# Loading V's weights on ScalarE's DMA queue instead of SyncE's, with four more idle products before the first transposes

## The chip, the cores and the metric

One core of a Trainium2 chip runs the whole program in one launch. The metric is the device time of that core in microseconds (us). The kernel before takes 897.44 us, the median of three runs that lie between 897.3 and 897.68 us.

## The reference: what is computed

The input x has 4 sequences of 512 tokens with 512 features. All arithmetic is float32.

```
xn = layernorm(x)                                # over the 512 features, no weights
q, k, v = xn @ wq.T, xn @ wk.T, xn @ wv.T        # 16 heads of q, 4 of k and v, 128 each; rope on q and k
per head, over chunks of tokens (linear attention with decay exp(-lam * distance)):
    o  = (q k^T * decay) v + (q * q_decay) kv
    kv = blk * kv + (k * k_decay)^T v
s = o @ wo.T
g = silu(mlp(xn))    # mlp: silu(xn @ gate * gs) * (xn @ up * us), then @ down * ds; weights rounded to fp8
out = x + s * g
```

## The kernel before, in words

Every matrix product is made from two or three passes over split operands: each float32 operand is split into a high part (a rounding cast by ScalarE) and a low part (the rest, by VectorE or GpSimd). The program has five instruction streams written out by hand, one for each engine, in a fixed order, and they meet at semaphores. No scheduler reorders them.

The stretch that the change touches is the first 30 us. The first sequence comes in four tiles of 128 tokens (`load_x`, into `stage`). For each tile VectorE takes statistics (`tile_stats`, L841), makes mean and variance (`mean_var`, L847 and L849), and after a power by GpSimd (`power`, L1285) the reciprocal deviation (`inv_std`, L857 to L863), and normalizes (`norm`, L876). The two tiles 0 and 1 form the first group, but VectorE's stream has `tile_stats(2)` between `mean_var(0)` and `inv_std(0)`. TensorE then turns each tile with four products against the identity `ident` (`ln_transpose`, L1428); ScalarE casts the turned tile (`norm_hi`, L576), VectorE makes its low part (`norm_lo`, L883). V's weights arrive in four pieces of 128 x 512 in `wv_raw`, which lies in the tile `f_all`. ScalarE casts them (`wv_split_hi`, L638), one piece ahead of `norm_hi(0)` and three behind it, and VectorE makes the low parts (`wv_split_lo`, L950). TensorE multiplies: `v_first_high` (L1392) for tiles 0 and 1 needs the casts of all four weight pieces and of the tile; `v_first_low` and `v_first_rest` (L1372) follow.

Ahead of the first transposes TensorE does `WARM` idle products on a zeroed tile, and `WARM_MORE` = 4 behind the second one; their results are never used. They are issued by this code (L1408):

```
pe.wait_ge(warm_d, 1)
warm_up(WARM)
pe.wait_ge(ident_sem, 16)
ln_transpose(0)
ln_transpose(1)
warm_up(WARM_MORE)
v_first_high(0)
v_first_high(1)
```

All loads and stores are issued by SyncE in one queue, in the order in which its stream is written: x tiles 0 to 3, `ident`, V's weights (L396), x tiles 4 to 7, the first pieces of the MLP's weights. Tiles 6 and 7 wait there until the `stage` slots of tiles 0 and 1 have been turned.

Of the kernel before, what the change touches and what calls it, by code (L numbers as in the profile page):

```python
# [17 lines left out]
KT = D // P  # L18
# [63 lines left out]
    for half in range(2):  # L82
        VD_AT[2 + (t + half) // MT, (t + half) % MT] = (x, half)
AW_FROM = 6
WARM = 14
WARM_MORE = 4


# [6 lines left out]
def attention_mlp_kernel(nc, x_nat, x_t, attn_w, wv_tab, out_w, mlp_w, scales, rope_tab, decay_tab, q_decay_tab,  # L95
                         k_decay_tab, ident_in, out):
    ctx = ExitStack()
    with ctx:
# [59 lines left out]
        wv_raw = f_all[:, MT - KT:MT, :]  # L158
# [95 lines left out]
        wv_in = [sem(f"wv_in{k}") for k in range(KT)]; wv_hi = sem("wv_hi"); wv_lo = sem("wv_lo")  # L254
# [49 lines left out]
        def _(sp):  # L304
# [87 lines left out]
            for i in range(TT):  # L392
                load_x(i)
            sp.dma_start(ident[:], ident_in).then_inc(ident_sem, 16)
            for k in range(KT):
                sp.dma_start(wv_raw[:, k, :], wv_tab[:, k, :]).then_inc(wv_in[k], 16)  # L396
            for i in range(TT, 2 * TT):
                load_x(i)
            load_piece(0)
# [172 lines left out]
        def _(act):  # L572
# [63 lines left out]
            def wv_split_hi(k):  # L636
                act.wait_ge(wv_in[k], 16)
                act.copy(wv[:, 0, k, :], wv_raw[:, k, :]).then_inc(wv_hi, 1)  # L638
# [15 lines left out]
            def vd_round(x, half):  # L654
                for g in (2 * half, 2 * half + 1):
# [3 lines left out]
                        act.wait_ge(vd_out[y % 2], 16 * (y // 2))  # L659
                    act.copy(vd_split[:, y % 2, 0, :], vd_sb[:, y % 2, :]).then_inc(vd_hi, 1)  # L660

            act.preload_act_table(ACT.Silu)
            wv_split_hi(0)
            norm_hi(0)
# [703 lines left out]
        def _(pe):  # L1368
# [36 lines left out]
            def warm_up(count):  # L1405

                for _ in range(count):
                    pe.matmul(bank[7][:], acc[:, 0, 0, 0:P // 2].bitcast(BF16), acc[:, 0, 0, 0:S // 2].bitcast(BF16),  # L1408
                              start=True, stop=True)
# [68 lines left out]
# [3 lines that stand above are left out]
# [272 lines left out]
```

## Time and profile before

| | |
|---|---|
| median of three runs | 897.44 us |
| the profiled execution's own time | 898.68 us |
| its span, first to last instruction | 896.9 us |
| TensorE busy in the span | 889.6 us (99%) |
| VectorE, ScalarE, GpSimd busy | 656.1, 409.5, 370.4 us |
| mean granted TensorE clock | 0.998 |

The profiled execution took 1.24 us longer than the median, and 1.8 us of it lie outside the span. A busy share near 99% says that TensorE nearly always had an instruction in flight; what it lacks are a few us, so the places to look at are those in which it is idle or runs at a lower clock.

### The profile page before, as it was taken

How to read it: one execution, taken by the hardware profiler on the slowest of the kernel's cores; microseconds unless marked ns; L12 is line 12 of the kernel's file. 1: busy time of each engine (PE TensorE's matmuls, PEld its weight loads, DVE VectorE, ACT ScalarE, POOL GpSimd, SP SyncE). 2: the span in 40 equal slices, each digit the busy share in tenths (PEclk: the TensorE clock that was granted, in tenths of full speed). 3: DMA queues.
4: the chain of work that ended last, by engine and by line, in shares of the span. 5: the costliest groups of instructions: out<-in, count | busy, mean ns of one | idle time of the engine just before them, and what ended most of it. 6: DMA issues, size and time to landing. Idle time of an engine off the chain costs nothing.

```text
span 896.9 us, 12455 instructions
## 1 busy us (share of the span) xinstructions
PE 889.6 (99%) x4060; PEld 735.0 (82%) x4060; DVE 656.1 (73%) x941; ACT 409.5 (46%) x683; POOL 370.4 (41%) x273
## 2 busy tenths in 40 slices
PE   8999999999999999999999999999999999999998
PEld 5888888888888888888888888888888888888887
DVE  6988896787643257766777867677767678788798
ACT  2544343443533455445355454463554544634442
POOL 1012112122122475536545456365454563553546
PEclk9999999999999999999999999999999999999999
DMA  6694414389650534522544614345335064273854
GB/s 215 187 390 167 171 48 164 141 307 328 244 211 1 212 125 147 186 80 108 187 126 156 220 39 175 102 175 194 101 144 181 18 221 160 99 259 103 295 135 169
DMA packets 86922, 150.08 MB, mean 167 GB/s; under 512 B 38480, under 2 KB 59616, under 8 KB 81504
## 3 DMA queue, kind: packets, MB, share of 16 engines
q1 hardware_dynamic: 86880, 149.55, 48.7%
q8 instruction: 23, 0.38, 0.2%
q14 instruction: 19, 0.16, 0.1%
HBM read 103.38 MB, written 46.15 MB: 167 GB/s over the span
## 4 chain that ended last, share of the span: by engine, by line
PE 91%; issue 3%; DVE 3%; POOL 2%; DMA 0%; ACT 0%; SPq 0%; DVEq 0%; POOLq 0%; ACTq 0%
PE bank L1372 90%; POOL d_r L1308 1%; POOL rot L1317 1%; DMA stage<-in_x_nat 0%; PE bank L1392 0%; DVE d_sb L1164 0%; DVE tail_sb L1217 0%; DVE d_sb L1116 0%; DVE tail_sb L1215 0%; DVE d_r L1191 0%; PE bank L1428 0%; DVE acc L1211 0%; PE bank L1408 0%; DVE o_r L1170 0%; DVE tail_sb L1201 0%
## 5 line engine op out<-in xcount | busy, mean ns | idle before, releaser
L1372 PE MATMUL bank<-xn,aw 128*128 128x512 f32 x960 | 229.1, 390 | 0.0
L1317 POOL TENSOR_TENSOR rot<-rot 128x512 f32<-128x512 f32 x80 | 126.7, 1583 | 233.4 <-DVE rot L1103 233.4
L1372 PEld LDWEIGHTS bank<-xn,aw 128*128 128x128 f32 x960 | 179.0, 188 | 37.4 <-issue 0.7
L1372 PE MATMUL bank<-o_r,ow 128*128 128x512 f32 (+1 forms) x792 | 184.5, 383 | 0.2 <-DVE o_r L1170 0.2
L1308 POOL TENSOR_TENSOR d_r<-d_sb,d_r 128x512 fp32r<-128x512 f32 x126 | 165.5, 1336 | 37.0 <-ACT d_r L762 36.9
L1372 PE MATMUL bank<-xn,gu_w 128*128 128x512 f32 x768 | 179.6, 389 | 0.0
L1372 PEld LDWEIGHTS bank<-o_r,ow 128*128 128x128 f32 x792 | 145.5, 188 | 29.8 <-issue 0.6
L1372 PEld LDWEIGHTS bank<-xn,gu_w 128*128 128x128 f32 x768 | 144.2, 188 | 29.9
L1102 DVE TENSOR_TENSOR rot<-bank,rope 128x512 f32<-128x512 f32 x80 | 55.2, 690 | 100.2 <-ACT rot L747 100.1
L746 ACT COPY rot<-bank 64x512 f32<-64x512 f32 x80 | 46.8, 584 | 156.9 <-PE bank L1372 156.6
L762 ACT CAST d_r<-d_sb 128x512 fp32r<-128x512 f32 x128 | 78.9, 621 | 83.2 <-DVE d_sb L1164 60.7
L1291 POOL TENSOR_TENSOR fsplit<-f_all,fsplit 128x512 fp32r<-128x512 f32 x36 | 49.0, 1366 | 129.1 <-ACT fsplit L620 129.1
L1372 PE MATMUL bank<-fsplit,dn_w 128*128 128x512 f32 x384 | 93.8, 390 | 0.0
L1372 PEld LDWEIGHTS bank<-fsplit,dn_w 128*128 128x128 f32 x384 | 71.8, 188 | 15.5 <-issue 0.3
L1116 DVE TENSOR_TENSOR d_sb<-rot,q_decay 128x256 f32<-128x256 f32 x64 | 83.6, 1324 | 1.2 <-POOL rot L1317 1.2
L1164 DVE TENSOR_TENSOR d_sb<-bank,decay 128x512 f32<-128x512 f32 x96 | 64.0, 684 | 22.5 <-PE bank L1372 21.5
L1372 PE MATMUL bank<-q_r,k_r 128*128 128x512 f32 x288 | 78.5, 391 | 0.0
L1372 PE MATMUL bank<-d_r,v_r 128*128 128x512 f32 (+1 forms) x336 | 76.8, 361 | 0.1
L1372 PEld LDWEIGHTS bank<-d_r,v_r 128*128 128x128 f32 x336 | 57.7, 188 | 13.1 <-POOL d_r L1308 2.3
L1372 PEld LDWEIGHTS bank<-q_r,k_r 128*128 128x128 f32 x288 | 52.9, 188 | 10.7 <-DVE q_r L1109 0.6
L735 ACT CAST q_r<-rot 128x512 fp32r<-128x512 f32 x64 | 39.8, 622 | 40.1 <-POOL rot L1317 39.0
L945 DVE SCALAR_TENSOR_TENSOR f_all<-bank,scale_sb,f_all 128x512 f32<-128x512 f32 x36 | 26.9, 748 | 41.5 <-PE bank L1372 36.0
(91 smaller groups left out, 948.9 us busy)
## 6 DMA issues: line engine op xcount, KB each, us to landing
xn<-xn_split SPq DMA_DIRECT2D x15, 2048.0 KB, 7.8
v_decayed<-vd_split SPq DMA_DIRECT2D x32, 512.0 KB, 3.2
vd_r<-v_decayed SPq DMA_DIRECT2D x16, 1024.0 KB, 7.0
v_r<-v_split SPq DMA_DIRECT2D x16, 512.0 KB, 3.5
wst<-in_mlp_w SPq DMA_DIRECT2D x10, 768.0 KB, 6.6
xn_split<-xn SPq DMA_DIRECT2D x3, 2048.0 KB, 13.3
stage<-in_x_t SPq DMA_DIRECT2D x20, 256.0 KB, 5.0
stage<-in_attn_w SPq DMA_DIRECT2D x4, 1280.0 KB, 5.5
```

The costliest lines, as they stand in the source:

```text
L735: act.copy(dst, rot1[:, r % RRING, :]).then_inc(qk_hi, 1)
L746: act.copy(rot2[0:ROT, r % RRING, :], ps[ROT:, :])
L762: act.copy(d_r[:, slot(e), 0, :], d_sb[:, slot(e), :]).then_inc(d_hi, 1)
L945: dve.scalar_tensor_tensor(out=f, in0=gu_ps[(2 * u + 1) % 3][:], scalar=scale_sb[:, MT + m:MT + m + 1], in1=f, op0=ALU.mult, op1=ALU.mult) ...
L1102: dve.tensor_tensor(rot1[:, r % RRING, :], proj_bank(n, r)[:], rope[:, 0, :], ALU.mult)
L1116: dve.tensor_tensor(d_sb[:, slot(e), bass.ts(h % 2, HALF)], rot1[:, (h + 1) % RRING, HALF:S], q_decay[:, h, :], ALU.mult).then_inc(q_decay ...
L1164: dve.tensor_tensor(by_head(d_sb[:, slot(e), :]), by_head(sc_ps[t % TRING][:]), decay[:, h0:h0 + nh, i0 - j:i0 - j + ni, :], ALU.mult).the ...
L1291: pool.tensor_tensor(fsplit[:, e % FRING, 1, :], src, fsplit[:, e % FRING, 0, :].bitcast(F32), ALU.subtract).then_inc(f_lo, 1)
L1308: pool.tensor_tensor(d_r[:, slot(e), 1, :], d_sb[:, slot(e), :], d_r[:, slot(e), 0, :].bitcast(F32), ALU.subtract).then_inc(d_lo, 1)
L1317: pool.tensor_tensor(rot1[:, r % RRING, :], rot1[:, r % RRING, :], rot2[:, r % RRING, :], ALU.add).then_inc(qk_sum, 1)
L1372: last = pe.matmul(dst, a, b, start=start and x == 0, stop=stop and x == len(pairs) - 1)
```

## The change

`WARM` goes from 14 to 18. SyncE's stream no longer issues the four loads of V's weights; ScalarE's stream issues them as its first instructions, ahead of its table load. No wait is added or removed.

```
-WARM = 14
+WARM = 18
             for i in range(TT):
                 load_x(i)
             sp.dma_start(ident[:], ident_in).then_inc(ident_sem, 16)
-            for k in range(KT):
-                sp.dma_start(wv_raw[:, k, :], wv_tab[:, k, :]).then_inc(wv_in[k], 16)
             for i in range(TT, 2 * TT):
                 load_x(i)
             load_piece(0)
...
+            for k in range(KT):
+                act.dma_start(wv_raw[:, k, :], wv_tab[:, k, :]).then_inc(wv_in[k], 16)
             act.preload_act_table(ACT.Silu)
             wv_split_hi(0)
             norm_hi(0)
```

SyncE's stream from its start, before and now (`f_all` is where V's weights land, `stage` takes the x tiles), as the difference:

```order
 L310 DMA stage<-in_x_nat 128x512 x4
 L394 DMA ident<-in_ident 128x128
-L396 DMA f_all<-in_wv_tab 128x512 x4
 L310 DMA stage<-in_x_nat 128x512 x4
 L338 DMA wst<-in_mlp_w 128x512 x2
```

The four weight loads are gone, and x tiles 4 and 5 stand right behind the identity. ScalarE's stream from its start, before (its table load, then the weight casts around the first cast of x):

```order
0 L571 UNCONDITIONAL_BRANCH
1 L662 ACT_TABLE_LOAD
2 L638 CAST wv<-f_all 128x512
3 L576 CAST xn<-bank 128x4x128
4 L638 CAST wv<-f_all 128x512 x3
5 L576 CAST xn<-bank 128x4x128 x3
```

And now, the same stretch of ScalarE:

```order
0 L569 UNCONDITIONAL_BRANCH
1 L661 DMA f_all<-in_wv_tab 128x512 x4
2 L662 ACT_TABLE_LOAD
3 L636 CAST wv<-f_all 128x512
4 L574 CAST xn<-bank 128x4x128
5 L636 CAST wv<-f_all 128x512 x3
6 L574 CAST xn<-bank 128x4x128 x3
```

The four issues come first; the casts keep their order, with three weight casts still behind the first cast of x. On TensorE only the count of the first group of idle products differs.

## Rows read from the trace of the kernel before

**Rows 1.** The page: busy time of the span, and the chain by line.

```profile
PE 889.6 (99%) x4060; PEld 735.0 (82%) x4060; DVE 656.1 (73%) x941; ACT 409.5 (46%) x683; POOL 370.4 (41%) x273
...
PE 91%; issue 3%; DVE 3%; POOL 2%; DMA 0%; ACT 0%; SPq 0%; DVEq 0%; POOLq 0%; ACTq 0%
```

**Rows 2.** Waits of TensorE from 26.2 us to the end: total, times, longest.

```profile
PE bank L1372 <- DVE o_r L1170: 0.2, 1, 0.2
```

**Rows 3.** Stretches: length, busy of each engine, PEclk, DMA share, GB/s.

```profile
0.00:9.20 9.20, 5.76 (x18) 2.29 (x19) 4.47 (x13) 1.90 (x2) 1.05 (x7) 1.00 0.72 234
9.20:9.30 0.10, 0.10 (x3) 0.10 (x2) 0.10 (x1) 0.00 (x0) 0.00 (x0) 0.89 0.96 369
9.30:12.60 3.30, 3.30 (x12) 2.17 (x10) 2.90 (x11) 2.62 (x5) 0.70 (x1) 0.50 0.81 253
12.60:12.70 0.10, 0.10 (x2) 0.06 (x1) 0.10 (x1) 0.00 (x0) 0.00 (x0) 0.54 0.52 164
```

**Rows 4.** Timeline of TensorE's start: start, length, instruction, count, idle before.

```profile
1.47 5.35 PE L1408 MATMUL bank<-acc 128*128 128x512 bf16 x14 [1.47 <-DVE acc L989]
8.79 1.49 PE L1428 MATMUL bank<-ident,stage 128*128 128x128 f32 x8 [1.97 <-DVE stage L876]
10.07 1.91 PE L1408 MATMUL bank<-acc 128*128 128x512 bf16 x4
11.43 2.79 PE L1392 MATMUL bank<-wv,xn 128*128 128x512 f32 x8
14.05 1.03 PE L1428 MATMUL bank<-ident,stage 128*128 128x128 f32 x8
```

**Rows 5.** Timeline of TensorE's weight loads for the first idle products.

```profile
5.29 0.15 PEld L1408 LDWEIGHTS bank<-acc 128*128 128x128 bf16 x1 [0.28 <-issue]
5.71 0.61 PEld L1408 LDWEIGHTS bank<-acc 128*128 128x128 bf16 x3 [0.28 <-issue]
```

**Rows 6.** Timeline of VectorE, 5.2 to 8.9 us.

```profile
5.43 0.69 DVE L841 BATCH_NORM_STATS2 stats<-stage 128x6 f32<-128x512 f32 x1 [0.82 <-DMA stage<-in_x_nat]
...
6.52 0.69 DVE L841 BATCH_NORM_STATS2 stats<-stage 128x6 f32<-128x512 f32 x1
7.51 0.16 DVE L857 TENSOR_TENSOR rs<-rs 128x2 f32<-128x2 f32 x1 [0.31 <-POOL rs L1285]
...
8.10 1.00 DVE L876 TENSOR_SCALAR stage<-stage,mv,rstd 128x512 f32<-128x512 f32 x2
```

**Rows 7.** Timeline of ScalarE, 8 to 13 us.

```profile
8.44 0.62 ACT L638 CAST wv<-f_all 128x512 fp32r<-128x512 f32 x1 [6.41 <-DMA f_all<-in_wv_tab]
9.46 0.59 ACT L576 CAST xn<-bank 128x512 fp32r<-128x512 f32 x1 [0.41 <-PE bank L1428]
9.95 1.66 ACT L638 CAST wv<-f_all 128x512 fp32r<-128x512 f32 x3
11.51 0.58 ACT L576 CAST xn<-bank 128x512 fp32r<-128x512 f32 x1
```

**Rows 8.** Timeline of SyncE's issues from the start.

```profile
0.75 1.82 SPq L310 DMA_DIRECT2D stage<-in_x_nat  x4
2.61 0.43 SPq L394 DMA_DIRECT2D ident<-in_ident  x1
3.09 1.92 SPq L396 DMA_DIRECT2D f_all<-in_wv_tab  x4
```

**Rows 9.** DMA issues one by one, in order of issue: size, us to landing.

```profile
stage<-in_x_nat SPq DMA_DIRECT2D x1, 256.0 KB, 3.1
...
stage<-in_x_nat SPq DMA_DIRECT2D x1, 256.0 KB, 4.2
...
stage<-in_x_nat SPq DMA_DIRECT2D x1, 256.0 KB, 4.4
...
stage<-in_x_nat SPq DMA_DIRECT2D x1, 256.0 KB, 5.4
...
ident<-in_ident SPq DMA_DIRECT2D x1, 64.0 KB, 5.2
...
f_all<-in_wv_tab SPq DMA_DIRECT2D x1, 256.0 KB, 5.5
...
f_all<-in_wv_tab SPq DMA_DIRECT2D x1, 256.0 KB, 5.8
```

**Rows 10.** Stretches, for the DMA engines: columns as in Rows 3.

```profile
2.00:7.00 5.00, 4.82 (x14) 1.59 (x12) 2.19 (x6) 0.03 (x1) 0.24 (x1) 1.00 0.85 254
7.00:10.00 3.00, 1.21 (x8) 1.24 (x9) 2.54 (x9) 1.16 (x3) 0.48 (x1) 0.88 1.03 388
```

More of the change, by code:

```diff
@@ L84 @@
 AW_FROM = 6
-WARM = 14
+WARM = 18
 WARM_MORE = 4
@@ L394, in _ @@
             sp.dma_start(ident[:], ident_in).then_inc(ident_sem, 16)
-            for k in range(KT):
-                sp.dma_start(wv_raw[:, k, :], wv_tab[:, k, :]).then_inc(wv_in[k], 16)
             for i in range(TT, 2 * TT):
@@ L660, in vd_round @@
                     act.copy(vd_split[:, y % 2, 0, :], vd_sb[:, y % 2, :]).then_inc(vd_hi, 1)
+            for k in range(KT):
+                act.dma_start(wv_raw[:, k, :], wv_tab[:, k, :]).then_inc(wv_in[k], 16)
             act.preload_act_table(ACT.Silu)
```

## The prediction

> **What bounds the kernel now.** I read the page first. TensorE is busy for 889.6 of 896.9 us and carries 91% of the chain that ended last; DMA and ScalarE have 0% of it [rows 1]. So only what moves TensorE's stream can move the end. Then I asked for TensorE's waits behind the stretch that the change touches: from 26.2 us on there is one, of 0.2 us [rows 2]. From there TensorE is the bound without a gap, and whatever is won or lost before 26.2 us is carried to the end one to one. I look for no second effect there.
>
> Before it, TensorE's timeline has two losses [rows 4]. The 14 idle products run from 1.47 to 6.82 us, then the engine stands for 1.97 us until VectorE has normalized tile 0, and the first transposes start at 8.79 us. The granted clock then falls from 1.00 (2.4 GHz) to 0.50 (1.2 GHz) near 9.3 us and stays there until just short of 12.7 us [rows 3]. Four idle products take 1.91 us in that stretch [rows 4]. At the very start the clock column says 1.00, but the loads of the idle products come 0.42 us apart (5.29 to 5.71) and only the last three stand within 0.61 us [rows 5]. So they too ran at the lower level until about 5.8 us, and an idle product costs about 0.43 us before and 0.21 us behind that point.
>
> What does the first transpose wait for? Going back: normalizing starts at 8.10, the last steps of the deviation at 7.51, and between them and the statistics of tile 1 (5.43, which waited for its tile) stand the statistics of tile 2 at 6.52 [rows 6]. So the chain is x tile 1, then x tile 2, then VectorE. Landing times are issue [rows 8] plus time to landing [rows 9]; the issues are some 0.47 us apart. X tiles 0 to 3 land at 3.9, 5.4, 6.1 and 7.6 us, the identity at 7.8, V's weight pieces at 8.4 (the start of the cast that waited for it, [rows 7]), 9.1, 9.7 and 10.3.
>
> **The change part by part.** *The weight loads come sooner.* ScalarE waited 6.41 us for the first piece, the largest wait at the start, and it looks like the prize. It is not on the path. That cast ends at 9.06, and ScalarE then waits another 0.41 us for TensorE's transposes before it casts x tile 0 at 9.46 [rows 7]. The other three weight casts stand behind that cast in ScalarE's stream, at 9.95 and after, back to back for 1.66 us. Pieces 2 to 4 had landed at 9.1, 9.7 and 10.3, each before its cast. Earlier weights are worth 0.0 us.
>
> *The four issues on ScalarE* should take what they take on SyncE, 1.92 us [rows 8], from about 0.75 us on. With the table load behind them ScalarE is free near 4 us, well before any cast has input. Cost 0; if that cover were gone it would be 1.9 us of ScalarE.
>
> *SyncE loses 1.92 us of issues* behind the identity. X tiles 4 and 5 are issued that much earlier; nobody asks for them until VectorE is done with the first sequence. The issues of tiles 6, 7 and the MLP weights wait for the transposes of tiles 0 and 1, so they move with those. Worth 0.
>
> *The x tiles get company.* This is the term that decides. Before, the x tiles were alone on the DMA engines until V's weights followed them. Now four weight loads of 256 KB are issued at the same moments. From 2 to 7 us the engines were already busy for 0.85 of the time while they moved only 254 GB/s, against 388 GB/s at a share of 1.03 in the 3 us behind [rows 10]. There is little idle DMA time to hide another 1 MB in. The bounds: at best the x tiles land as before (0 us); at worst each x tile is one half of a stream of twice the bytes. Then x tile 0 takes the place of the second load in the old order (5.4 us), tile 1 that of the fourth (7.6), tile 2 that of the sixth (9.1 less the 0.25 us of the identity, 8.8), tile 3 that of the eighth (10.05), the identity follows at 10.3. The statistics of tile 2 then run from 8.8 to 9.5. The power by GpSimd is done by then, so the 0.31 us wait is gone, and the steps from 7.51 to 8.10 (0.59 us) and from 8.10 to the first transpose at 8.79 (0.69 us) follow: 10.8 us. The first transpose is 2.0 us later than before. I take this end, because the share of 0.85 is near to full.
>
> The Trainium skill (DMA: Bandwidth & Descriptors, section Queues, rings and completion order) says that SyncE's and ScalarE's queues are rings on the same 16 engines and that each engine takes turns between rings packet by packet. No row of the trace shows two such queues at once. By that rule the sum takes the 2.0 us; the hope that a second queue brings the weights for free would give 0.
>
> *Four more idle products.* They run behind the 14 at 0.21 us each, from 6.82 to about 7.7 us. With the old start at 8.79 us they lie wholly in the idle time, and would cut it to 1.1 us. With the new start at 10.8 they leave 3.1 us idle, more than the 1.97 us behind which the clock fell before. They delay nothing; what they can do is hold the clock.
>
> *What the clock is worth.* From the first transpose to the second pair at 14.05 took 5.26 us. At full clock ScalarE sets the pace: its cast of x starts 0.67 us behind the first transpose (9.46), the last cast of that row ends 2.63 us later (12.09), and four products at some 0.235 us (0.94) follow: 4.24 us, 1.0 less. Should the lower level already be there when work starts and end about 12.7 us as before, the first four transposes take 0.85 instead of 0.67 us and the rest still goes by ScalarE: 0.2 us worse. So the clock gives back 0.8 to 1.0 us in both cases, because less work falls into the slow stretch.
>
> **The sum.** +2.0 for the later start, -0.9 for the section behind it, 0 for the rest: +1.1 us. I round it up to +1.2, since the mechanism's other details (issues that share their hardware) can only add. Against the profiled execution's 898.68 us that is 899.9; this execution stood 1.24 us above the median, so the median should come out at 898.6 us.
>
> **The rivals.** *Slower: the late start meets the low clock in full.* Price: if the clock falls half a microsecond behind the first transpose and stays down 3.4 us, as it did before, nothing is given back, and the whole 2.0 us stays. If it stays down through the eight products of the first pair, eight transposes at half speed (1.7 us), four idle products (1.7) and eight products at 0.43 (3.4) end at 17.6 instead of 14.05 us: +3.6. I take +2.5, 899.9 us. It decides against me once the low level overlaps more than about 3 us of the work behind the first transpose. For it speaks that the idle gap grows from 2.0 to 3.1 us; against it, that the four more products keep TensorE busy longer ahead of the gap.
>
> *The tiles don't feel the company.* Their requests are ahead or the second queue fills the gaps; the start stays at 8.79, the idle time shrinks to 1.1 us, and the clock holds. Then the section takes 4.24 us instead of 5.26: -1.0 us, 896.4. For it speaks the low rate of the first microseconds, 254 GB/s, which more requests might lift; against it the busy share of 0.85.
>
> *The start stays and the clock falls all the same.* Nothing changes: 897.4 us. It needs the same luck with the tiles, and an idle time of 1.1 us that still costs the clock.
>
> **How the numbers follow.** My forecast 0.58, centred at 898.6 with 897.8 to 899.1 as its own range (a half shared start to a full one). The slower rival 0.26, the one with the clock held 0.11, the last 0.05. What a measurement of this kernel can tell from no change is about 0.2%, 1.8 us. The forecast lies wholly inside that, the slower rival mostly outside (0.25 of its 0.26), with 0.02 for more delay than I priced: slower 0.27. The gain of 1.0 us is inside as well; for faster over 1.8 us the clock and more would have to come back, 0.03. Same is 0.70. The range takes in the held clock below, 896.5, and most of the slower rival above, 900.6.
>
> **What would show it.** In the profile of the changed kernel: the landing of x tile 2, and with it the second statistics behind the start, near 8.8 us instead of 6.1; the first transpose between 10 and 11 us instead of 8.79, with an idle time before it of about 3 us; the weight casts still in the same places behind the first cast of x; the granted clock low for less work than before; and from 26 us on the same rows moved by the same amount. If the first transpose still stands at 8.8 us, the sharing of the DMA engines is wrong and the sign of the sum with it. If it is late but the second pair of transposes is more than 1.8 us behind 14.05, it was the clock.

## The result, and the profile after

The changed kernel takes 903.6 us, the median of six runs (903.16 to 904.69), against 897.64 us before in the same runs; the ratio is 1.0067 with a 95% interval of 1.0056 to 1.0077. I had forecast 898.6 us, with 900.6 as the upper end. The sign was right and the size was five times too small: +6.0 us instead of +1.2. I had given 0.27 to a loss of more than 1.8 us. The profiled execution of the changed kernel, 904.69 us, is the slowest of the six, 1.1 us above their median.

The page of the changed kernel has the chain by line and, new, a second queue (q10 is ScalarE's):

```profile
span 902.6 us, 12463 instructions
...
q1 hardware_dynamic: 86304, 148.50, 48.0%
q10 hardware_dynamic: 576, 1.05, 0.4%
...
PE bank L1372 90%; POOL d_r L1308 1%; DMA stage<-in_x_nat 1%; POOL rot L1317 1%; PE bank L1392 1%; DVE d_sb L1164 0%; DVE tail_sb L1217 0%; DVE d_sb L1116 0%; DVE tail_sb L1215 0%; PE bank L1428 0%; DVE d_r L1191 0%; DVE acc L1211 0%; PE bank L1408 0%; DVE o_r L1170 0%; DVE tail_sb L1201 0%
```

The load of x has reached the chain with 1%, where DMA had 0% [rows 1]. TensorE's start, to be held against [rows 4] (start, length, instruction, count, idle before):

```profile
1.47 5.76 PE L1408 MATMUL bank<-acc 128*128 128x512 bf16 x18 [1.47 <-DVE acc L989]
13.15 1.94 PE L1428 MATMUL bank<-ident,stage 128*128 128x128 f32 x8 [5.92 <-DVE stage L876]
14.89 1.91 PE L1408 MATMUL bank<-acc 128*128 128x512 bf16 x4
16.24 3.30 PE L1392 MATMUL bank<-wv,xn 128*128 128x512 f32 x8
19.38 1.04 PE L1428 MATMUL bank<-ident,stage 128*128 128x128 f32 x8
```

The first transpose starts at 13.15 us instead of 8.79, and the second pair at 19.38 instead of 14.05. The idle time before the first is 5.92 us. VectorE, against [rows 6], shows what it waited for:

```profile
6.16 0.69 DVE L841 BATCH_NORM_STATS2 stats<-stage 128x6 f32<-128x512 f32 x1 [4.75 <-DMA stage<-in_x_nat]
9.64 0.69 DVE L841 BATCH_NORM_STATS2 stats<-stage 128x6 f32<-128x512 f32 x1 [2.78 <-DMA stage<-in_x_nat]
...
11.28 0.69 DVE L841 BATCH_NORM_STATS2 stats<-stage 128x6 f32<-128x512 f32 x1 [0.46 <-DMA stage<-in_x_nat]
...
12.46 1.00 DVE L876 TENSOR_SCALAR stage<-stage,mv,rstd 128x512 f32<-128x512 f32 x2
```

Tile 0 comes at 6.1 us instead of 3.9, tile 1 at 9.6 instead of 5.4, tile 2 at 11.3 instead of 6.1. The issues themselves, against [rows 8]:

```profile
0.76 2.74 SPq L310 DMA_DIRECT2D stage<-in_x_nat  x4
3.54 2.13 SPq L394 DMA_DIRECT2D ident<-in_ident  x1
```

```profile
0.75 2.77 ACTq L661 DMA_DIRECT2D f_all<-in_wv_tab  x4
3.55 1.28 ACT L662 ACT_TABLE_LOAD   x1 [3.55 <-issue]
6.35 0.62 ACT L636 CAST wv<-f_all 128x512 fp32r<-128x512 f32 x1 [1.51 <-DMA f_all<-in_wv_tab]
14.28 0.58 ACT L574 CAST xn<-bank 128x512 fp32r<-128x512 f32 x1 [7.31 <-PE bank L1428]
14.76 1.66 ACT L636 CAST wv<-f_all 128x512 fp32r<-128x512 f32 x3
```

Four issues take 2.74 and 2.77 us on the two queues at the same time, where SyncE alone needed 1.82, and that of the identity takes 2.13 instead of 0.43. Only the first piece of the weights comes sooner, at 6.3 us instead of 8.4, and nobody uses it: ScalarE casts it at 6.35 and then waits 7.31 us for the transposes. The other three land at 9.8, 11.4 and 12.7 us, which is 0.8, 1.7 and 2.3 us later than before. The stretches answer to [rows 3] and [rows 10] (length, busy of the engines, granted clock, DMA share, GB/s):

```profile
2.00:5.00 3.00, 3.00 (x9) 1.07 (x8) 0.00 (x0) 1.28 (x1) 0.00 (x0) 1.00 0.84 130
5.00:7.00 2.00, 2.00 (x11) 0.79 (x9) 0.69 (x1) 0.62 (x1) 0.00 (x0) 1.00 0.75 214
...
11.90:18.60 6.70, 5.45 (x17) 4.13 (x18) 6.08 (x19) 2.63 (x5) 0.70 (x1) 0.50 0.45 131
```

Two rows to notice. From 2 to 5 us the DMA engines are as busy as before, 0.84, and move 130 GB/s; before, that stretch moved 230 at a share of 0.80. And the granted clock stands at 0.50, the level of 1.2 GHz, from about 11.8 to 18.6 us, for twice as long as before, over nearly all of the work between the two pairs of transposes.

From 31.4 us on the timelines of the two profiled executions run side by side as forecast, 5.3 us apart up to the first products of the MLP's down weights (64.17 us against 58.85). At the end they are 5.7 us apart. Both executions are slower than the median of their kernel by more than a microsecond.

### The profile page after: what moved, and what is told of

Same layout as the page of the kernel before. It is cut to its first block, busy times and chain, and to the rows that moved or that the text cites. A ratio compares the mean times of both kernels' runs of the same rounds, so it can differ in the third digit from the quotient of the medians.

```text
span 902.6 us, 12463 instructions
## 1 busy us (share of the span) xinstructions
PE 891.2 (99%) x4064; PEld 736.1 (82%) x4064; DVE 655.5 (73%) x941; ACT 409.0 (45%) x683; POOL 370.6 (41%) x273
## 4 chain that ended last, share of the span: by engine, by line
PE 91%; issue 3%; DVE 3%; POOL 2%; DMA 1%; ACT 0%; SPq 0%; DVEq 0%; POOLq 0%; ACTq 0%
PE bank L1372 90%; POOL d_r L1308 1%; DMA stage<-in_x_nat 1%; POOL rot L1317 1%; PE bank L1392 1%; DVE d_sb L1164 0%; DVE tail_sb L1217 0%; DVE d_sb L1116 0%; DVE tail_sb L1215 0%; PE bank L1428 0%; DVE d_r L1191 0%; DVE acc L1211 0%; PE bank L1408 0%; DVE o_r L1170 0%; DVE tail_sb L1201 0%
## 5 line engine op out<-in xcount | busy, mean ns | idle before, releaser
L1372 PEld LDWEIGHTS bank<-q_r,k_r 128*128 128x128 f32 x288 | 52.9, 188 | 10.8 <-DVE q_r L1109 0.6
```

The lines of the kernel that those rows point to most:

```text
L1372: last = pe.matmul(dst, a, b, start=start and x == 0, stop=stop and x == len(pairs) - 1)
```

## The experiments

All times are medians in us, next to the kernel before timed on the same chip: 897.48 for the first four experiments, 897.69 for the next four, 897.67 for e9 to e11 and 897.47 for e12. "Tile 2" is its landing, "start" the first transpose, both from the profile; the rate is that of 2 to 5 us.

| | queues in use at the start | tensors read first | GB/s | tile 2 | start | time | ratio to before, 95% |
|---|---|---|---|---|---|---|---|
| before | 1 | x, then weights | 230 | 6.1 | 8.79 | | |
| changed | 2 | x and weights | 130 | 11.3 | 13.15 | 903.6 | 1.0056 to 1.0077 |
| e1 | 2 | x and weights | 130 | 10.9 | 13.03 | 903.5 | 1.0056 to 1.0089 |
| e2 | 1 | x, then weights | 231 | 6.4 | 8.61 | 897.83 | 0.9993 to 1.0012 |
| e3 | 1 | x and weights | 162 | 8.3 | 11.66 | 901.73 | 1.003 to 1.0063 |
| e4 | 1, then 2 | x, then weights | 242 | 5.9 | 8.86 | 900.63 | 1.0023 to 1.0045 |
| e5 | 2 | x and weights | 134 | 11.1 | 13.39 | 902.81 | 1.0044 to 1.0078 |
| e6 | 2 | x | 283 | 6.0 | 8.80 | 897.82 | 0.9993 to 1.0012 |
| e7 | 2 | x and 1/4 weights | 136 | 7.8 | 10.49 | 901.37 | 1.0024 to 1.0052 |
| e8 | 1, ScalarE's | x, then weights | 248 | 6.1 | 8.12 | 897.5 | 0.9988 to 1.0007 |
| e9 | 2 | x and a copy of x | 150 | 8.9 | 10.77 | 901.09 | 1.0024 to 1.0049 |
| e10 | 1 | x and a copy of x | 165 | 6.8 | 9.24 | 898.88 | 1.0001 to 1.0021 |
| e11 | 2 | x with weights behind it | 295 | 8.4 | 10.26 | 901.02 | 1.0022 to 1.005 |
| e12 | 1 | x tiles apart, then weights | 315 | 5.8 | 7.68 | 897.08 | 0.9988 to 1.0006 |

**e1: the move alone.** `WARM` back to 14 in the changed kernel.

> The move of V's weight loads alone, with 14 idle products as before. If the queue is the whole cause (my theory now), x tile 2 lands near 11.3 us as in the changed kernel, the first transpose is at about 13.1 us, and the time is 903.6 us within 0.7. If the four more idle products had a part in the loss, it comes out over 1 us below 903.

903.5 us, start at 13.03. The move is the whole loss; no part of the four idle products in it can be seen. This profile, 903.36 us, lies beside the median of its kernel, so it tells of the usual run better than that of the changed kernel does:

```profile
13.03 1.94 PE L1428 MATMUL bank<-ident,stage 128*128 128x128 f32 x8 [6.38 <-DVE stage L876]
...
17.96 1.03 PE L1428 MATMUL bank<-ident,stage 128*128 128x128 f32 x8
```

The stretch at the lower level, columns as above:

```profile
9.00:15.70 6.70, 2.67 (x11) 2.09 (x12) 5.20 (x17) 1.55 (x4) 1.42 (x2) 0.50 0.52 196
```

The clock is at 0.50 for as long as in the changed kernel's profile, but it fell about 3 us sooner, while TensorE still stood idle. Only 2.7 us of work fall into the slow stretch, and the second pair of transposes comes 4.93 us behind the first instead of 6.23.

**e2: the idle products alone.** `WARM` to 18 in the kernel before.

> The four more idle products alone, all loads on SyncE as before. Both theories leave the first transpose at 8.8 us. If the shorter idle time of 1.1 us holds the clock, the second pair of transposes starts near 13.0 instead of 14.05 us and the time is 896.4 to 896.9 us. If the clock falls all the same, it is 897.6 us, no change.

```profile
1.47 5.64 PE L1408 MATMUL bank<-acc 128*128 128x512 bf16 x18 [1.47 <-DVE acc L989]
8.61 1.06 PE L1428 MATMUL bank<-ident,stage 128*128 128x128 f32 x8 [1.50 <-DVE stage L876]
...
12.99 1.04 PE L1428 MATMUL bank<-ident,stage 128*128 128x128 f32 x8
```

In this profile the clock held and the second pair came at 12.99 us, as expected of a held clock, yet the median says no change. The two agree once the single runs of the kernel before are read: in the 17 of them timed beside e1 to e4 the span is 895.4 to 896.1 us in 15, with a granted clock of 0.999 or 1.0 in all of these. The profiled execution of before, 896.9 us at 0.998, was one of the few with so low a mean clock. The idle products have next to nothing to win in the usual run.

**e3: one queue, the same order.**

```
             for i in range(TT):
                 load_x(i)
+                sp.dma_start(wv_raw[:, i, :], wv_tab[:, i, :]).then_inc(wv_in[i], 16)
             sp.dma_start(ident[:], ident_in).then_inc(ident_sem, 16)
-            for k in range(KT):
-                sp.dma_start(wv_raw[:, k, :], wv_tab[:, k, :]).then_inc(wv_in[k], 16)
```

> One queue (SyncE's), but the x tiles and V's weight pieces are issued in turn: x 0, weights 0, x 1, weights 1 and so on, then the identity. Theory A (two queues in flight at once slow the first transfers down): with one queue the engines keep their rate of some 250 GB/s, x tile 2 lands near 8.8 us, the first transpose is at 10.8 us, and the time is 898.7 to 899.6 us. Theory B (only the order of the bytes counts, whoever issues them; two tensors read for the first time at once are slow): x tile 2 lands near 11 us and the time is about 903 us, as with the second queue. The issues reach at most 0.5 us later than with two queues.

```profile
11.66 1.97 PE L1427 MATMUL bank<-ident,stage 128*128 128x128 f32 x8 [5.05 <-DMA ident<-in_ident]
```

Between the two theories. Tile 2 lands at 8.3 us, near the 8.8 us that the order alone gives, and 3 us sooner than with two queues; but the rate from 2 to 5 us is down to 162 GB/s with one queue too, and the identity, last in the line at 11.6 us, becomes what the transposes wait for. The time, 901.73 us, lies between both. The lower rate looks different here: the busy share of the DMA engines is 0.56, where the changed kernel has 0.84.

**e4: ScalarE's queue, but later.** `act.wait_ge(x_in[0], 16)` ahead of ScalarE's four issues in e1.

> ScalarE's queue as in the changed kernel, but ScalarE waits for x tile 0 (landed 3.9 us before) and only then issues the four weight loads, at about 3.9 to 5.8 us instead of SyncE's 3.1 to 5.0; 14 idle products. Theory A says that the second queue hurts from the moment that it has work: tile 0 lands at 3.9 us, tiles 1 and 2 and the identity are delayed by 1 to 3 us, and the time is 899 to 902 us. Theory B says that what hurts is that the weights stand ahead of the x tiles; here three x tiles are issued before them, so x tile 2 lands within 0.7 us of the 6.1 us of before, and the time is 897.6 to 899 us.

```profile
8.86 1.50 PE L1429 MATMUL bank<-ident,stage 128*128 128x128 f32 x8 [1.98 <-DMA ident<-in_ident]
...
12.55 3.23 PE L1393 MATMUL bank<-wv,xn 128*128 128x512 f32 x8 [0.48 <-ACT xn L574]
```

```profile
4.06 3.37 ACTq L662 DMA_DIRECT2D f_all<-in_wv_tab  x4
...
11.39 0.62 ACT L636 CAST wv<-f_all 128x512 fp32r<-128x512 f32 x1 [2.64 <-DMA f_all<-in_wv_tab]
```

```profile
6.00:8.00 2.00, 0.88 (x4) 0.20 (x2) 1.55 (x8) 0.53 (x1) 0.71 (x1) 1.00 0.75 122
```

Neither theory had this. Tiles 0 to 2 keep their times, as the second had it; tile 3 and the identity are 1 us late, and the time lies in the range of the first. But what costs the time is that now the weights are late. Their first piece lands 7.3 us after its issue, at 11.4 instead of 8.4, the cast of x tile 0 stands behind it in ScalarE's stream, and TensorE waits for that. The loss has changed its place, 3.1 us by the medians. A part of the delay is the order, since x tiles 4 and 5 now stand ahead of the weights. Another part is a slow phase, and it comes late: from 6 to 8 us (the last fence), with the loads of the weights in flight beside those of x, the engines move 122 GB/s, where before that stretch moved 344.

**e5: the clock held in the changed kernel.** `WARM` to 46.

> The changed kernel with 46 idle products instead of 18: at 0.21 us each they reach from 1.5 to about 13 us, so that TensorE has no long idle time before its first transposes at about 13.1 us. My theory: of the 6 us about 4.4 are the later first transpose and some 1.5 the clock that falls in the longer idle time. Then the granted clock stays at 1.00, the stretch from the first to the second pair of transposes takes about 4.4 us (it was 6.2), and the time is 901.8 to 902.3 us. The rival, that the clock has no part and all comes from the loads: 903.5 us, or more if the products run past the arrival of the data.

```profile
1.47 12.08 PE L1408 MATMUL bank<-acc 128*128 128x512 bf16 x46 [1.47 <-DVE acc L989]
13.39 1.04 PE L1428 MATMUL bank<-ident,stage 128*128 128x128 f32 x8
...
17.74 1.03 PE L1428 MATMUL bank<-ident,stage 128*128 128x128 f32 x8
```

With no idle time the granted clock stays at 1.00 and the section takes 4.35 us instead of 6.23. The time falls from 903.6 to 902.81 us, half of what I expected: the clock has a part of about 0.8 us, and the intervals of the two ratios overlap. The profile of the changed kernel overstates it, since it is the slowest of six; e1's, beside its median, has 4.93 us for that section, 0.6 us more than here.

**e6: two queues, but x alone.** SyncE issues tiles 0 and 2, ScalarE 1 and 3; the weights stay on SyncE.

```
-            for i in range(TT):
+            for i in (0, 2):
                 load_x(i)
...
+            for i in (1, 3):
+                act.dma_start(stage[:, NAT[i], :], x_nat[ORDER[0], :, i, :]).then_inc(x_in[NAT[i]], 16)
             act.preload_act_table(ACT.Silu)
```

> Two queues with only x tiles at the start: SyncE issues tiles 0 and 2, ScalarE tiles 1 and 3; V's weights stay behind the identity on SyncE as before. Theory A (two queues in flight slow the first transfers whatever they carry): the rate from 2 to 5 us falls to 110 to 170 GB/s from 250, x tile 2 lands 1 to 3 us after the 6.1 us of before, and the time is 899 to 901 us. Rival C (two queues are slow only where they read two tensors at once): the rate stays near 250 GB/s, x tile 2 lands at 5.5 to 6.3 us and the time is 897 to 898 us.

```profile
2.00:5.00 3.00, 3.00 (x9) 1.07 (x8) 0.15 (x1) 0.96 (x1) 0.00 (x0) 1.00 0.93 283
5.00:7.00 2.00, 2.00 (x7) 0.56 (x5) 1.93 (x6) 0.00 (x0) 0.23 (x1) 1.00 1.04 359
```

283 GB/s and no loss. My theory, that two queues in flight slow the first transfers, falls here.

**e7: a quarter of the dose.** Only weight piece 0 on ScalarE's queue, the others on SyncE behind the identity.

> Only the first of the four weight pieces on ScalarE's queue at once, the other three on SyncE behind the identity; 14 idle products. If the loss grows with the bytes that share the first microseconds, it is about a quarter to a half of the 6 us: x tile 2 lands near 7.0 to 7.5 us, the first transpose is at 9.7 to 10.2 us, the time is 898.5 to 900.5 us. If any use of the second queue brings the whole loss, x tile 2 lands over 9 us and the time is over 901.5 us.

```profile
2.00:5.00 3.00, 3.00 (x9) 1.04 (x8) 0.00 (x0) 0.47 (x1) 0.00 (x0) 1.00 0.85 136
5.00:7.00 2.00, 1.79 (x7) 0.49 (x5) 0.56 (x1) 0.38 (x1) 0.00 (x0) 1.00 0.97 335
```

One piece is enough to bring the rate from 2 to 5 us down to 136 GB/s, close to the full dose's 130; from 5 us on it is back at 335. So the slow phase is an entrance fee, not a price per byte. Tile 0 lands at 6.4 us instead of 3.9, and tile 2 at 7.8, a little beyond what I expected; so is the time, 901.37 us. That is 3.7 us of loss with a start only 1.9 us later than e2's: the other 1.9 us are the clock, which stands at 0.50 from 9.2 to 16.0 us, so that the section up to the second pair takes 6.26 us instead of e2's 4.38.

**e8: one queue, ScalarE's.** X tiles, identity and weights issued by ScalarE in the old order; SyncE waits for tile 3 before it goes on.

> One queue, but ScalarE's: x tiles 0 to 3, the identity and V's weights are issued by ScalarE in the old order, and SyncE waits for x tile 3 before it issues x tiles 4 to 7 and the rest. If ScalarE's queue is as good as SyncE's, and the loss is from two queues at once, x tile 2 lands at 6.1 us within 0.5 and the time is 897.2 to 898.2 us. If the loss is a slower ScalarE queue, x tile 2 lands beyond 7 us and the time is 899 us or more.

248 GB/s, tile 2 at 6.1 us, 897.5 us: ScalarE's queue is as good as SyncE's.

**e9 and e10: a second tensor with x's own bytes.** `x_copy` is a second input, equal to the first sequence. e9 is e6 with ScalarE's tiles read from it:

```
-                act.dma_start(stage[:, NAT[i], :], x_nat[ORDER[0], :, i, :]).then_inc(x_in[NAT[i]], 16)
+                act.dma_start(stage[:, NAT[i], :], x_copy[0, :, i, :]).then_inc(x_in[NAT[i]], 16)
```

> The kernel with x tiles 0 and 2 on SyncE and 1 and 3 on ScalarE, which lost nothing, but ScalarE reads its two tiles from a second input, a copy of the first sequence. Same bytes, queues, issues and order; only the memory region that tiles 1 and 3 come from is another. Theory C (what is slow is to start two tensors in memory at once): the rate from 2 to 5 us falls from 283 to 130 to 180 GB/s, x tile 2 lands over 1 us later than the 6.2 us of that kernel, and the time is 899 to 901.5 us. Rival D (only V's weights, their bytes in front, or the order count): tile 2 lands at 6.2 us within 0.4 and the time is 897.8 us.

```profile
2.00:5.00 3.00, 3.00 (x11) 1.12 (x10) 0.00 (x0) 0.96 (x1) 0.00 (x0) 1.00 0.87 150
```

e10 is the kernel before, on one queue, with tiles 1 and 3 from the copy:

```
+                src = x_copy[0] if i in (1, 3) else x_nat[ORDER[i // TT]]
-                sp.dma_start(stage[:, NAT[i], :], x_nat[ORDER[i // TT], :, i % TT, :]).then_inc(x_in[NAT[i]], 16)
+                sp.dma_start(stage[:, NAT[i], :], src[:, i % TT, :]).then_inc(x_in[NAT[i]], 16)
```

> The kernel before, all on SyncE's queue, but x tiles 1 and 3 are read from the copy. It parts the two tensors from the two queues. Theory C: the rate from 2 to 5 us falls below 200 GB/s from some 240, and the tiles land late with one queue too: tile 2 at 6.8 to 8 us, the time 898.5 to 900 us. If it takes two queues and two tensors together, tile 2 lands at 6.1 us within 0.4 and the time is 897.6 us.

```profile
2.00:5.00 3.00, 3.00 (x11) 1.08 (x10) 0.21 (x1) 0.03 (x1) 0.00 (x0) 1.00 0.68 165
```

This pair, with e6 and before, is the cleanest of the study: the same bytes, destinations and issues, and only the source moves. The rate goes from 283 to 150 GB/s on two queues and from 230 to 165 on one. It costs 3.4 us on two queues and 1.2 on one, as the theory of two tensors had it. Of the 3.4, 0.9 us are the clock, by the profile.

**e11: the weights in x's tensor.** The move as changed, with 14 idle products, and V's weights in the megabyte right behind the first sequence of x.

```
+    wv_tab = x_wv[ORDER[0] + 1]
+    x_nat = [x_wv[s + (s > ORDER[0])] for s in range(NB)]
```

> The move of V's weights to ScalarE's queue as changed (14 idle products), but the weights lie in the same tensor as x, in the megabyte right behind the first sequence. If being another tensor (far away in memory) is what is slow, most of the loss goes: x tile 2 lands near 8.8 us, where my sum had it, the first transpose is near 10.8 us and the time is 899 to 900.5 us. If any second region of 1 MB counts, near or far, it is 903.5 us as with the weights in a tensor of their own.

```profile
2.00:5.00 3.00, 3.00 (x10) 1.08 (x9) 0.32 (x1) 1.42 (x2) 0.00 (x0) 1.00 0.93 295
```

```profile
10.26 1.06 PE L1430 MATMUL bank<-ident,stage 128*128 128x128 f32 x8 [4.10 <-DMA ident<-in_ident]
11.16 1.70 PE L1410 MATMUL bank<-acc 128*128 128x512 bf16 x4
12.30 3.35 PE L1394 MATMUL bank<-wv,xn 128*128 128x512 f32 x8
15.49 1.04 PE L1430 MATMUL bank<-ident,stage 128*128 128x128 f32 x8
```

The rate is back, at 295 GB/s. Tile 2 lands at 8.4 us and the start is at 10.26; the sum of the prediction had 8.8 and 10.8. The transposes wait for the identity, which lands at 10.2 us, but VectorE has finished tile 0 only just before, so both bounds lie close together. 2.6 us of the changed kernel's 6.0 are gone. The time, 901.02 us, is half a microsecond above what I expected.

**e12: each x tile in one piece.** The kernel before, with the first sequence's tiles in an input where each is 256 KB in a row.

> The kernel before, with the four tiles of the first sequence in an input of their own in which each tile is one contiguous stretch of 256 KB (before, each tile took 2 KB out of every 8 KB of a megabyte). Same queue, order and bytes. If what is slow is the first read of a stretch of memory, and it goes by how much memory a load is spread over, tile 0 and tile 1 land sooner (3.5 and 4.6 us instead of 3.9 and 5.2 to 5.4), the first transpose comes up to 0.7 us sooner and the time is 897.0 us within 0.3: a version that beats both. If it goes by how many stretches are opened, tiles 1 to 3 each open one: the rate from 2 to 5 us stays at or below 240 GB/s and the time is 897.7 to 899 us.

```profile
7.68 1.06 PE L1429 MATMUL bank<-ident,stage 128*128 128x128 f32 x8 [0.25 <-DVE stage L877]
...
9.52 3.24 PE L1393 MATMUL bank<-wv,xn 128*128 128x512 f32 x8
12.60 1.04 PE L1429 MATMUL bank<-ident,stage 128*128 128x128 f32 x8
```

315 GB/s, and the start 0.9 us sooner than in e2. The second pair of transposes gains only 0.4 us on e2's, since the weights still land at 8.3 us and ScalarE's first weight cast is now what the chain waits for. The median is 0.4 us below before, but the interval of 0.9988 to 1.0006 does not tell it from no change. It fits the first reading (a load spread over less memory starts faster) and is no proof of a better kernel.

## Why the prediction was wrong

*What bounds the kernel, and what carries over*: right in the main. TensorE is the bound from 26 us on, and most of the shift is there when the first tile sequence is done. But I looked for no second effect behind it, and 0.5 to 0.9 us come there in the changed kernel and e1 (the table below).

*Earlier weights are worth 0*: right as a value. Three of the four casts still stand behind the first cast of x, and ScalarE waits 7.31 us for TensorE. But the premise was wrong for three pieces of four: they land 0.8 to 2.3 us later than before.

*The x tiles get company, +2.0 us*: this is the step that failed, by its size. The start moved by 4.4 us (13.15 us against 8.79; e1 against e2, 13.03 against 8.61). Its mechanism, an order in which each x tile shares with a weight piece, is right and was sized well: e11, where the rate is not down and the sharing is left, has the start at 10.26 us, 1.65 us behind e2's. That is the Trainium skill's rule (DMA: Bandwidth & Descriptors, Queues, rings and completion order), that the engines take turns between rings, and e11's trace agrees with it: tile 2 at 8.4 us against 8.8 by the turns. What the step left out is that I took the landing times of the old order, in which one tensor after the other is opened, for a stream from two. Opening x and the weights together costs another 2.8 us of start (e1's 13.03 against 10.26) and 2.6 us of time. I also read the DMA share of 0.85 [rows 10] as a measure of room. From 2 to 5 us it went from 0.80 to 0.84 while the bytes fell to almost half. And I put tile 2 on the path of the kernel before, where its statistics start at 6.52 us without a wait for it [rows 6]; in the changed kernel they do wait, 0.46 us.

*The issues on ScalarE cost 0*: right as to ScalarE's own work, which has no use for the time. But they took 2.77 us and not the 1.92 that they take on SyncE alone: with slow transfers the fourth issue and the identity's waited.

*The clock gives back 0.9 us*: wrong in sign. There was nothing to give back, because the execution profiled before was an unusual one, while most runs beside it have a granted clock of 0.999 to 1.0. My sum took that time off twice, as 0.9 us for the clock and again within the 1.24 us by which that execution stood above the median. And the slower rival's mechanism did occur: after 5.92 us of idle time nearly all the work between the pairs of transposes ran at 1.2 GHz, and the section took 6.23 us instead of e2's 4.38. Its part in the usual run is 0.6 us by e1's profile and about 0.8 by e5's median. The sign I had named for it would have misled me: I wrote that it was the clock if the second pair stood more than 1.8 us behind 14.05. It stands 5.3 us behind, and 4.4 of these come from the later start.

*The idle products delay nothing and hold nothing*: right, by e1 and e2.

*Where the 6 us are.* Each row is one profiled execution against e2's, in us; e2's was 897.53 us, beside the medians of both its kernel and the one before. "Section" goes from the first transpose to the second pair, and what it adds is the clock, but for e4 and e12, which are left out. "Behind" is all the rest.

| | later start | longer section | behind | together |
|---|---|---|---|---|
| changed | 4.5 | 1.85 | 0.5 | 6.9 |
| e1 | 4.4 | 0.55 | 0.9 | 5.9 |
| e3 | 3.05 | 1.2 | 0.1 | 4.4 |
| e5 | 4.8 | 0 | 0.45 | 5.2 |
| e7 | 1.9 | 1.9 | 0 | 3.8 |
| e9 | 2.2 | 0.9 | 0 | 3.1 |
| e11 | 1.65 | 0.85 | 0.4 | 2.9 |

The part behind goes with waits of TensorE's weight loads behind 31.5 us that the profile puts down to "issue" (us in total, times, longest; e2, the changed kernel, e1):

```profile
PEld bank L1372 <- issue: 1.9, 6, 0.6
PEld bank L1372 <- issue: 2.4, 7, 0.6
PEld bank L1372 <- issue: 2.9, 8, 0.6
```

E3, e7 and e9 have six of these and nothing to speak of behind the section; e5 and e11 have seven, like the changed kernel. So the usual run's 6.0 us are, by e1, 1.65 us of start by the shared order, 2.8 by two tensors at once, some 0.55 of clock and 0.9 in two such waits. What ends these waits, and why they come only in the kernels that issue all four weight pieces on ScalarE's queue from the start, is not shown.

## What to carry to other kernels

Ask of a load that comes earlier who waits for it in its engine's own order; here the consumer stood behind the very tiles that the earlier load delayed. In the first microseconds give the tensor on the critical chain the DMA engines to itself, and try what must come with it in the same tensor; one run, e11, speaks for that, and it still lost 3.35 us against the kernel before. Before a forecast of about a microsecond is built on one profiled execution, hold its span and mean clock against those of the other runs; here the profiled executions of both kernels stood more than 1 us above their medians.

## What the runs showed that I had not expected

Reading two tensors at once in the first microseconds brings the DMA engines from 230 to 315 GB/s down to 130 to 165 in every kernel that did it (changed, e1, e3, e5, e7, e9, e10), by one queue or by two, and for as little as one load of 256 KB. On two queues the engines stay busy meanwhile, with a share of 0.76 to 0.87; on one the share falls as well, to 0.56 (e3) and 0.68 (e10), against 0.80 before, so it is open whether the two cases have one cause. Both in one tensor, one behind the other, kept 295 (e11). What in the memory path does it, and whether the distance or the tensor counts, is not settled: e11 changed both. It isn't bound to the first packets of the program: in e4, which opens the weights at 4.1 us, the slow stretch comes from 6 to 8 us. Later than that it wasn't tried.

The length of TensorE's idle time alone does not tell whether the clock falls. In e10 it stood for 3.23 us before the first transposes and the granted clock kept 1.00 behind them; in the profile before it stood for 1.97 us, and the clock fell to 0.50.

The clock column at a program's start can mislead: it says 1.00 from 0 us on, while the idle products come 0.43 us apart up to 5.8 us [rows 5], which is the lower level, and 0.21 us behind that point.
